# State product of the scan as one stacked product, context result kept on chip, last cell block closed in the next stage

## The reference, cut to what matters

```
x = x + xattn(norm(x), ctx_1024, ctx_1024, mask, ...)   # stage mask
x = x + attn(norm(x), context, ...)                      # stage wide
x = x + ffn0(norm(x), ew, ..., ln_g, ln_b)               # stage cell: six nodes, closes with norm(out)*g + b
x = x + softmax(norm(x) @ ctx^T) @ ctx                   # stage context attention
x = x + scan(norm(x), A, W_b, b_b, W_c, b_c, D, W_t, b_t, W_o, b_o)
x = x + ffn1(norm(x), ...)                               # 8-bit weights plus low rank, gelu
```

```
delta = sigmoid(xn @ W_t^T + b_t) * 0.99 + 0.01
Bu    = xn @ W_b^T + b_b                     # 16 states
h[t]  = exp(A*delta[t]) * h[t-1] + Bu[t]     # along the 64 tokens of a row
y     = (h @ W_c^T + b_c + xn * D) @ W_o^T + b_o
```

## Time and profile before

| what | value |
|---|---|
| median of 3 runs | 2986.65 us (2983.41 to 2986.8) |
| profiled execution, its own time | 2986.81 us |
| its span in the trace | 2985.1 us |
| PE busy | 2840.7 us (95%), 32038 matmuls |
| DVE, ACT, POOL busy | 2157.8, 2034.8, 1176.5 us |
| mean granted TensorE clock | 0.983 |

### The profile page before, as it was taken

How to read it: one execution, slowest core, us unless ns; L and a number is a source line. 1 busy time by engine, 2 the same in 40 slices (tenths; PEclk the granted TensorE clock), 3 DMA queues, 4 the chain that set the end, 5 groups by cost and what they waited for, 6 DMA issues and landing times. The chain is left out here.

```text
span 2985.1 us, 84625 instructions
## 1 busy us (share of the span) xinstructions
PE 2840.7 (95%) x32038; PEld 2213.5 (74%) x32038; DVE 2157.8 (72%) x5328; ACT 2034.8 (68%) x4128; POOL 1176.5 (39%) x962
## 2 busy tenths in 40 slices
PE   8999999799999999999999999999999998789999
PEld 6888888566666666666687888887888887556798
DVE  7888888777777767777637777787778776668443
ACT  6888888787777777787616766766676666333444
POOL 6777777576665556666500010011010000211310
PEclk9999999999999999999989999999999999889899
DMA  4111111167778788787851002112011122660000
GB/s 151 52 60 51 60 51 47 26 134 151 149 165 157 160 165 163 160 175 156 195 187 48 33 31 73 38 45 71 22 45 52 52 80 76 211 224 25 8 22 29
DMA packets 622398, 283.51 MB, mean 95 GB/s; under 512 B 549356, under 2 KB 598439, under 8 KB 621879
## 3 DMA queue, kind: packets, MB, share of 16 engines
q1 hardware_dynamic: 602134, 235.35, 32.5%
q10 hardware_dynamic: 19968, 44.05, 4.2%
HBM read 123.59 MB, written 21.50 MB: 49 GB/s over the span
## 5 line engine op out<-in xcount | busy, mean ns | idle before, releaser
L1538 POOL TENSOR_TENSOR front_parts<-front_prob,front_parts 128x1024 f16<-128x1024 f32 x256 | 545.7, 2132 | 328.3 <-ACT front_parts L1746 292.0
L1836 DVE TENSOR_REDUCE wide_row_max<-wide_score 128x1 f32<-128x1024 f32 x256 | 312.4, 1220 | 125.0 <-PE wide_score L1579 124.5
L1734 ACT ACTIVATE front_prob<-wide_score,wide_neg_max,front_s_up 128x1024 f32<-128x1024 f32 x256 | 307.5, 1201 | 124.6 <-DVE wide_neg_max L1839 118.7
L1579 PE MATMUL wide_score<-wide_kT,wide_qT 128*128 128x512 f16 x1536 | 374.5, 380 | 7.0 <-ACT front_prob L1734 5.5
L2144 POOL TENSOR_TENSOR cell_w<-cell_w_stage,cell_w 128x1536 fp32r<-128x1536 f32 x23 | 80.4, 3495 | 643.7 <-ACT cell_w L2412 643.7
L847 POOL TENSOR_TENSOR common_common<-common_common,mask_inv_sum 128x512 f32<-128x512 f32 x256 | 271.8, 1062 | 108.5 <-DVE mask_inv_sum L1245 105.9
L1102 ACT ACTIVATE common_common<-common_common,mask_row_min 128x256 f32<-128x256 f32 x512 | 254.9, 502 | 48.1 <-DVE mask_row_min L1193 47.8
L1746 ACT ACTIVATE front_parts<-front_prob 128x1024 f16<-128x1024 f32 x256 | 270.0, 1055 | 14.6 <-ACT front_prob L1734 7.2
L1579 PEld LDWEIGHTS wide_score<-wide_kT,wide_qT 128*128 128x128 f16 x1536 | 144.3, 98 | 154.5 <-ACT front_prob L1734 7.7
L2605 DVE TENSOR_REDUCE cell_row_max<-cell_score 128x8 f32<-128x512 f32 x192 | 131.0, 682 | 157.8 <-PE cell_score L2242 155.2
L1193 DVE CUSTOM_DVE_ANT_0 common_common<-mask_score,front_prob 128x256 f32<-128x256 f32 x512 | 189.1, 416 | 3.6 <-issue 3.6
(11 more groups left out here) (349 smaller groups left out, 6581.1 us busy)
## 6 DMA issues: line engine op xcount, KB each, us to landing
cell_w_stage<-cell_weights ACTq DMA_DIRECT2D x24, 768.0 KB, 5.1
front_cT<-in_ctx_turned SPq DMA_DIRECT2D x32, 512.0 KB, 3.3
ahead_home<-in_ctx_odd SPq DMA_DIRECT2D x16, 1024.0 KB, 7.4
cell_w_stage<-in_L_ffn_W_own ACTq DMA_DIRECT2D x24, 512.0 KB, 3.6
front_prob<-in_mask_BxS_ik SPq DMA_DIRECT2D x32, 256.0 KB, 3.6
front_probT<-front_parts SPq DMA_TRANSPOSE x512, 2.8
ahead_home<-in_ctx_even SPq DMA_DIRECT2D x16, 512.0 KB, 5.6
common_common<-in_L_ffn_W_pairs SPq DMA_DIRECT2D x10, 512.0 KB, 4.4
```

The lines of the kernel that those rows point to most:

```text
L1538: pool.tensor_tensor(parts[:, s % 2, LO, :], prob[:, s % 2, :], parts[:, s % 2, HI, :], ALU.subtract).then_inc(part_lo, 1)
L1579: mm = pe.matmul(score[:, s % 2, half * 512:(half + 1) * 512], qT[:, u_par, a, s * P:(s + 1) * P], kT[:, par, b, half * 512:(half + 1) * 5 ...
L1734: act.activation(prob[:, s % 2, :], score[:, s % 2, :], ACT.Exp, bias=neg_max[:, s % 2:s % 2 + 1], scale=s_up[:, 0:1], accum_out=row_sum[: ...
L1836: dve.tensor_reduce(row_max[:, one], score[:, s % 2, :], AX.X, ALU.max).then_inc(max_found, 1)
```

## The change

1. **Cell's last closing.** finish() of block 7 is no longer run in the cell stage. `z`, `x_res`, `g_row` and the norm's buffers move into ContextFront, and VectorE runs the four parts of the close at the end of context steps 1, 2, 3 and 4 (finish_block); ScalarE stores the block at step 5. The norm of context units 0 and 1 moves the other way, into the cell stage's last slot. The store of block 6 stands behind the copies of block 7 out of the accumulator.
2. **Context result on chip.** The result of each unit goes straight to `x_all`, which now lies over the cell's `common` buffer; the 32 stores of the context stage and the loads of `x` in the scan stage are gone. The scan's twelve weight loads are issued at the start of the context stage into the first 2640 floats of the node buffer, and for that five of the eight first contexts are loaded later in the cell stage (after the accumulation of node 4). `keep_clock` at the context's start is 6 transposes, before 24; the one at the scan's start is gone. The norm of block 0 of the scan runs in context steps 30 and 31.
3. **State product.** `state` (16 states and a row of ones) is split in two float32r parts, leading (ScalarE, twice: rows 0 to 16 and 64 to 80 of `state_stack`) and remaining (GpSimd, rows 32 to 48); `w_stack` holds leading, leading and remaining parts of `w_state` at the same rows. One float32r product 81 rows deep takes the place of the float32 product 17 rows deep.

```diff
+    def vector_finish_norm(self, dve, blk):
+
+        self.last_norm.vector_apply(dve, blk, self.z, False, self.z)
+
+    def vector_finish_scale(self, dve, blk):
+
+        dve.wait_ge(self.last_norm.xn_ready, blk + 1)
+        dve.tensor_tensor(self.z[:, :, :], self.z[:, :, :], self.g_row[:, :].unsqueeze(1).to_broadcast([P, SUB, D]), ALU.mult).then_inc(self.z_step, 1)
+
+    def vector_finish_add(self, dve, blk, X):
+        dve.wait_ge(self.res_ready, blk + 1)
+        dve.wait_ge(self.z_step, blk + 1)
+        dve.tensor_tensor(self.x_res[:, X], self.x_res[:, X], self.z[:, :, :], ALU.add).then_inc(self.out_ready, 1)
+
+    def store(self, act, blk, X):
+        act.wait_ge(self.out_ready, blk + 1)
+        act.dma_start(block_rows(self.x_in[rows(blk * BLK, BLK), :]), self.x_res[:, X]).then_inc(self.x_stored[X], 16)
...
+    def load(self, sp):
+        A, W_b, b_b, W_c, b_c, D_skip, W_t, b_t, W_o, b_o = self.sources
+        N, w_loaded = self.N, self.w_loaded
+        col = lambda v: v.rearrange("(n a) -> n a", a=1)
+        sp.dma_start(self.wo[:, :, :], W_o.rearrange("(t p) i -> p t i", p=P)).then_inc(w_loaded, 16)
...
-        for k in (0, 2, 3):
-            ahead.load_context(sp, k // 2, k)
+        ahead.load_context(sp, 0, 0)
         sp.wait_ge(proj_ready, proj_at(i, 3, 1) + PROJ_SLOT)
         for k in (1, 5):
             ahead.load_context(sp, k // 2, k)
         sp.wait_ge(acc_ready, (attention(i, 4, 1) + 1) * DH)
-        for k in (4, 6, 7):
+        for k in (2, 3, 4, 6, 7):
             ahead.load_context(sp, k // 2, k)
...
+            if last:
+                for k in range(2):
+                    ahead.gpsimd_rstd(pool, k, k)
+            for X in range(1 if last else 2):
                 last_norm.gpsimd_rstd(pool, i * 2 + X)
...
-                if final and X == 1:
-                    store(i, 0)
                 if other:
...
+                if final and X == 1:
+                    ahead.store(act, i * 2, 0)
...
-            last_norm.vector_apply(dve, blk, z, False, z)
-
-            dve.wait_ge(last_norm.xn_ready, blk + 1)
-            dve.tensor_tensor(z[:, :, :], z[:, :, :], g_row[:, :].unsqueeze(1).to_broadcast([P, SUB, D]), ALU.mult).then_inc(z_step, 1)
-            dve.wait_ge(res_ready, blk + 1)
-            dve.wait_ge(z_step, blk + 1)
-            dve.tensor_tensor(x_res[:, X], x_res[:, X], z[:, :, :], ALU.add).then_inc(y_ready, 1)
+            ahead.vector_finish_norm(dve, blk)
+            ahead.vector_finish_scale(dve, blk)
...
+                if final and X == 1:
+                    for k in range(2):
+                        ahead.vector_stats(dve, k, k)
+                        ahead.vector_apply(dve, k, k)
...
+        scan_front.load(sp)
+        sp.wait_ge(front.x_stored[1], 16 * (NBLK // 2 - 1))
+        sp.wait_ge(front.x_stored[0], 16 * (NBLK // 2))
+        with sp.Fori(1, UNITS // NBUF - 1) as i:
             for k in range(NBUF):
                 load(i * NBUF + k, k, i * (NBUF // 2) + k // 2)
+        sp.wait_ge(front.x_stored[1], 16 * (NBLK // 2))
+        for u in range(UNITS - NBUF, UNITS):
+            load(u, u % NBUF, u // 2)
 
     @block.gpsimd
...
-        units(pool, store, lambda: None)
+        def step(u, k):
+            if not isinstance(u, int) or u >= 2:
+                front.gpsimd_rstd(pool, u, k)
+            if isinstance(u, int) and u == 3:
+                front.last_norm.gpsimd_rstd(pool, NBLK - 1)
+
+        scan_front.gpsimd_zero(pool)
+        units(pool, step, lambda: scan_front.norm.gpsimd_rstd(pool, 0))
...
-        keep_clock(pe, ident, out_ps, 24)
+        keep_clock(pe, ident, out_ps, 6)
...
-                dve.wait_ge(y_stored[j], 16 * ((u - j) // 2) if isinstance(u, int) else (u - j) * 8)
-
-            dve.scalar_tensor_tensor(y_sb[:, j, :], out_ps[:, 0:D], inv_sum[:, j:j + 1], x_sb[:, k, :],
+            dve.scalar_tensor_tensor(x_all[:, rows(u, 1), :].rearrange("p s d -> p (s d)"), out_ps[:, 0:D], inv_sum[:, j:j + 1], x_sb[:, k, :],
...
+            if isinstance(u, int) and u < NBUF:
+                finish_block(u)
+            if isinstance(u, int) and u == UNITS - 2:
+                dve.wait_ge(y_ready, SUB)
+                scan_front.norm.vector_stats(dve, 0, x_all[:, 0:SUB, :])
+            if isinstance(u, int) and u == UNITS - 1:
+                scan_front.norm.vector_apply(dve, 0, x_all[:, 0:SUB, :], False)
...
+        def finish_block(u):
+
+            blk = NBLK - 1
+            if u == 1:
+                front.last_norm.vector_stats(dve, blk, front.z)
+            if u == 2:
+                front.vector_finish_norm(dve, blk)
+            if u == 3:
+                front.vector_finish_scale(dve, blk)
+            if u == 4:
+                front.vector_finish_add(dve, blk, 1)
+
...
+    PARTS = (0, 32, 64)
+    STACK = PARTS[2] + N + 1
+    state_stack = mem.sb("state_stack", [STACK, 2, BLK], F32R)
+    w_stack = mem.sb("w_stack", [STACK, D], F32R)
...
-        sp.dma_start(of_block(0), block_rows(x_in[0:BLK, :])).then_inc(x_loaded[0], 16)
-        sp.wait_ge(zeroed, 2)
...
+        pool.memset(w_stack[:, :].bitcast(F32), 0.0).then_inc(zeroed, 1)
+        pool.memset(state_stack[:, :, :].bitcast(F32), 0.0).then_inc(zeroed, 1)
+        for n in range(1, 3):
             norm.gpsimd_rstd(pool, n)
+
+        def rest_of_state(n):
+            pool.wait_ge(state_hi, n * 2 + 1)
+            pool.tensor_tensor(part_of(state_stack, 1)[:, n % 2, :], state[:, n % 2, :], part_of(state_stack, 0)[:, n % 2, :].bitcast(F32),
+                               ALU.subtract).then_inc(state_lo, 1)
+            pool.wait_ge(state_lo, n + 1)
+
+        pool.wait_ge(zeroed, 4)
+        pool.wait_ge(norm.rstd_ready, 3)
+        rest_of_state(0)
+        for n in range(NBLK - 1):
+            if n + 3 < NBLK:
+                norm.gpsimd_rstd(pool, n + 3)
+                pool.wait_ge(norm.rstd_ready, n + 4)
+            rest_of_state(n + 1)
         ffn.gpsimd_lo(pool, 0, ffn.loras)
 
     @block.tensor
     def _(pe):
-        keep_clock(pe, ident, ffn_banks[0], 24)
...
-        keep_clock(pe, ident, ffn_banks[0], 24)
+        norm.tensor_turn(pe, 0, False)
...
-            pe.wait_ge(state_done, n + 1)
+            pe.wait_ge(state_hi, n * 2 + 2)
+            pe.wait_ge(state_lo, n + 1)
...
-                    mm = pe.matmul(dst, state[:, j, s * P:(s + 1) * P], w_state[:, :], start=False, stop=True)
+                    mm = pe.matmul(dst, state_stack[:, j, s * P:(s + 1) * P], w_stack[:, :], start=False, stop=True)
...
+        def leading_of_state(n):
+            act.wait_ge(state_done, n + 1)
+            if n >= 2:
+
+                act.wait_ge(out_ready, (n - 1) * 2)
+            for x in (0, 2):
+                act.activation(part_of(state_stack, x)[:, n % 2, :], state[:, n % 2, :], ACT.Copy).then_inc(state_hi, 1)
...
+            if follows(n, 1):
+                leading_of_state(n + 1)
...
-            dve.tensor_tensor(w_state[:, :], out_banks[0][0:N + 1, 0:D], bo_row[:, :], ALU.add).then_inc(prep_done, 1)
+            dve.tensor_tensor(w_state[:, :], out_banks[0][0:N + 1, 0:D], bo_row[:, :], ALU.add).then_inc(prep_step, 1)
+            dve.wait_ge(zeroed, 4)
+            dve.wait_ge(prep_step, 3)
+            for x in range(2):
+                ins = dve.tensor_copy(part_of(w_stack, x), w_state[:, :])
+            ins.then_inc(prep_step, 1)
+            dve.wait_ge(prep_step, 4)
+            dve.tensor_tensor(part_of(w_stack, 2), w_state[:, :], part_of(w_stack, 0).bitcast(F32), ALU.subtract).then_inc(prep_done, 1)
...
-                dve.wait_ge(out_ready, (n - 1) * 2)
+                dve.wait_ge(state_hi, (n - 1) * 2)
+                dve.wait_ge(state_lo, n - 1)
...
-        for n in range(3):
-            stats_of(n)
-            if n:
-                copy_lo(n - 1)
-            norm.vector_apply(dve, n, of_block(n), n > 0)
-            if n == 0:
-                prepare()
+        stats_of(1)
+        copy_lo(0)
+        prepare()
+        norm.vector_apply(dve, 1, of_block(1), True)
+        stats_of(2)
+        copy_lo(1)
+        norm.vector_apply(dve, 2, of_block(2), True)
```

248 lines of the change are left out of this document (127 added, 121 removed).

## The result

The changed kernel took 2959.65 us (median of 4 runs, 2957.16 to 2962.25) against 2985.23 for the kernel before in the same comparison (4 runs, 2983.41 to 2986.8): a ratio of 0.9916, 95% interval 0.9901 to 0.9932. That is 25.6 us less; 20.4 less was forecast (2966, range 2957 to 2975).

What follows compares the result with a forecast made beforehand. TensorE was taken to bound the context stage, TensorE and VectorE in turn the scan. Terms of -12.3, -2.1, +4.2, -1.3, -7.5, -2.9 and +1.5 sum to -20.4: from 2986.81 to 2966.4 us, range 2957 to 2975.

Steps and rivals of the forecast that it cites:

- Handover: Cell to context: TensorE's first transpose moves from 2551.86 to 2539.55 us, -12.3.
- Clock: Context start: 18 fewer transposes save 3.2 us, partly given back at the low clock level, leaving -2.1.
- fourth rival: Context stage: TensorE stays at the 1.2 GHz level after only six transposes; 3011 us if half the units do, chance 0.02.
- Close of block 7: Context steps 1 to 4: VectorE's 5.64 us of close work delays the row maxima of units 2 to 5, +4.2.
- lower bound of 2.1: Close in the context steps: the cost left of 5.64 us if all VectorE idle in four steps is used.
- Leaving the context: Context to scan: two clears and no store landing replace a store's issue, landing and three clears; -1.3 in all.
- Start of the scan: Scan start: first input projection at 8.4 us instead of 15.89, VectorE preparing from about 4.0; -7.5.
- second rival: First projection at 12 us, close at its full 5.64, two units at the low clock; 2974 us, chance 0.12.
- state product: Scan: one stacked product saves TensorE 0.48 us per output slice, mostly hidden behind VectorE; net -2.9.
- GpSimd's port: Scan: VectorE loses time beside GpSimd's eight subtractions through shared ports; +1.5, bounds 0 to 3.7.
- The prediction's own sign of this: Scan: VectorE's L325 or tensor_scalars stretched beside GpSimd's L3182 by over 1 us would show the forecast wrong.
- The gain of the steps in the middle: Scan step 3 and the next: VectorE's wait for TensorE shrinks, about -1.6.

Runs made afterwards that it cites:

- e12: The kernel before with one edit, ScalarE's store of cell block 6 placed behind its copies of block 7 out of the accumulator; 2983.25 us, ratio 0.9993.
- e6: The changed kernel with block 7's close and its store back in the cell stage; 2966.97 us, ratio 0.9937.
- e7: The changed kernel with 24 transposes for the clock at the context's start in place of 6; 2963.19 us in one execution.
- e10: e9 without any transposes for the clock at the context's start; 2957.22 us, ratio 0.9911.
- e5: The changed kernel with block 7's close at context steps 1, 3, 5 and 6 and its store at step 7; 2958.75 us, ratio 0.9914.
- e2: The changed kernel with the float32 state product of before, without stacked parts, their copies or GpSimd's subtraction; 2960.29 us, ratio 0.992.
- e3: The changed kernel with the subtraction of state parts on VectorE in place of GpSimd; 2961.86 us, ratio 0.9921.
- e9: The changed kernel with the stacked state product for block 7 alone, w_stack made on ScalarE and GpSimd, first input projection released early; 2955.74 us, ratio 0.9903.

## Why the prediction was right, and where it was off

**Handover, right.** -12.75 for -12.3. The runs split it: the order of the store 2.8 (e12), the close 7.8 (18.91 to 11.10, e6), and what is left, 21.09 to 18.91 = 2.2, goes to the norm of two units ahead, by subtraction. The norm fits the gap, as assumed: VectorE's idle ahead of its last cell_oT part fell from 5.06 to 1.24.

**Clock, right.** -2.26 for -2.1. With the 24 it would be 1.5 to 2.5 longer (e7), and the six could not go too (e10). The fourth rival is out: the granted clock is 1.00 in the loop.

**Close of block 7, right in size, wrong in its reason.** +3.38 for +4.2. The lower bound of 2.1 rested on all of "0.89" idle per unit being of use, 3.56 in four units. Of the 5.64 the packed parts hid 2.3; spread over six units they hid 1.7 (e5), so that more free units don't collect more of it.

**Leaving the context, right.** -2.34 for -2.1, and the statistics of block 0 cost nothing (the maximum of unit 29 to the last result, 11.38 before, takes 11.44).

**Start of the scan, right.** -8.25 for -7.5: VectorE begins to prepare at 2.9, not 4.0. In executions where TensorE starts at the lower level the gain is 7.4. The second rival, with the projection at 12 and the close at its full 5.64, is out.

**Scan, the steps that failed.** The state product was to give -2.9 and GpSimd's port to take +1.5, -1.4 in all; measured -0.1. The port term was mis-sized: +3.5, close to its upper bound of 3.7, and not the 1.5 taken. The prediction halved the bound because no row showed the direction; the earlier trace rows showed GpSimd held by VectorE, and e2 and e3 show VectorE held by GpSimd as well. The prediction's own sign of this, L325 stretched by more than 1 us, was missed by 0.03.

The gain of the steps in the middle did come: 8.46 between two scans for 9.24, with L299's 0.86 already in it, and 9.20 for 9.40 ahead of that, 1.8 for 1.6 forecast. The next two intervals lost 0.80 and 1.03 to L314 and the first L325. The chain of the first outputs cost 1.27 in the first two intervals (4.78 and 9.46 for 4.25 and 8.72), where 0.6 was forecast.

The last block gave 2.4 where 1.9 was forecast, but by other sums: its four output slices gave 2.7 (2.5 against e2), since a slice saved 0.7 and not 0.48, the second L325 took 0.96 back, and 0.6 more came from work that no term touches: the sixteen products of L363 at its end, for one, took 5.91 before and 4.10 after. That the scan as a whole came within 1.3 of its forecast is in part luck: the port's 2.0 too much and the chain's 0.7 were made up in part by slices that saved more than assumed and by that last stretch.

The Trainium skill, page "SBUF — State Buffer", section "SBUF: two separate sides", calls the shared pair of ports an exclusive lock, held for the whole instruction by whichever starts first. The trace agrees in this, that VectorE is held too, by 0.76 on L314 (one operand) and by 0.95 and 0.97 on L325 (two operands). The total is that of the prediction's upper bound, but not its count: four holds of 0.76 to 0.97 in place of three of 1.24. Whether L314 and L299 ran in a two-port mode no run shows. In one place the order doesn't fit: the seventh subtraction is recorded 0.3 ahead of an L323 that took 2270 ns, as before (2271), and it was the subtraction that took 3722.

**What no term had.** 2.69 of the 24.6 come before the handover: 3.86 gained in the cell stage less 1.18 lost ahead of it. Without them the profile's sum is -21.9 for -20.4. By terms the profiled execution fell 4.2 below the forecast: cell stage 2.7, close 0.8, start 0.75, last result 0.6, handover 0.45, leaving 0.2, clock 0.2, less the scan's 1.3 and the end's 0.2. The median lies 2.6 below the profiled execution (2962.25), the slowest of its four, and the two make the 6.8 between 2966.4 and 2959.65. The sum had the mechanism of every large term right, and the time still fell near the lower end of the range, mostly by what no term had.

## What to carry to other kernels

A barrier between stages is worth attacking with whatever can be moved past it, even onto the engine that then becomes tight: 7.8 us of exposed latency cost 3.4 when spread among running work. Making TensorE faster where VectorE bounds the loop wins only in the block where nothing hides it; use the costlier preparation there alone (e9) and leave the rest as it was. When a helper goes to GpSimd beside a saturated VectorE, look at what VectorE runs beside each of its instructions: four of eight cost VectorE 0.76 to 0.97 us, about 60 to 80% of what the instruction takes alone, and those beside a reduction cost nothing.

## What the runs showed of the hardware

- GpSimd's subtraction of 17x512 takes 1252 to 1292 ns where VectorE doesn't hold it and up to 3722 ns beside a VectorE operation with two SBUF operands. The VectorE operation behind or beside it takes 0.76 to 0.97 us longer, and so does one of only two partitions (2x128, 217 to 1079 ns); a 128x2048 reduction doesn't. On VectorE the same subtraction takes 682 ns (e3).
- After 5.36 us idle at the same barrier TensorE's granted clock differs by what comes next: with six transposes ahead of the first scores it is 0.82 over the eleven us from the first turn; with none, 0.53 (e9, e10).
- From the first scan to the last the granted clock is 1.00 with the float32 state product (before, e2, e9, e10, e12) and 0.90 with the stacked one and its subtraction on GpSimd (the changed kernel and seven others). TensorE has less to do there and runs part of it at the lower level; no run isolates what that costs.
- The same last block of the scan ran at 0.50 over twelve us in one execution (e12), and its section was 5.6 us longer: a section that TensorE bounds has to be compared at the same clock.
- The cell stages of these programs differ by 2.0 and 2.5 us of 925 between kernels of the two kinds on one chip, one execution each; between the kernel before and the changed one the lead is there ahead of the first edited instruction.
